# Attention and ternary FFN layer on one core: x's second part held behind wkv, wkv turned in two halves, six warming products

## The reference

```python
x = x + xattn(layernorm(x), ctx_512, Wq, Wkv_expand, Wout)   # 16 heads of 16, softmax, causal
x = x + ffn(layernorm(x), w_gate, w_up, w_down)
# xattn: qp = q @ Wq.T ; kv = ctx @ Wkv_expand.T ; k, v = split(kv) ; causal keeps the first 56 context rows
#        out = softmax(mask(qh @ kh.T / 4)) @ vh ; out @ Wout.T
# ffn:   w -> round(w / mean|w|) clipped to -1..1 ; activations -> round(x * 127 / max|x|) per token
#        down(silu(gate) * up), each product with ternary weights and integer activations
```

## Time and profile before

| | before |
|---|---|
| median of three runs | 96.84 us (96.61 to 97.01) |
| the profiled execution | 97.0 us, of which the span is 95.3 |
| PE / DVE / ACT / POOL busy in the span | 83% / 72% / 60% / 54% |
| first weight transpose of Wq on PE (wqT) starts | 8.03 us |
| scores of slot 0 start | 11.96 us |

### The profile page before, as it was taken

How to read it: one execution, slowest core, us unless ns; L and a number is a source line. 1 busy time by engine, 2 the same in 40 slices (tenths; PEclk the granted TensorE clock), 3 DMA queues, 4 the chain that set the end, 5 groups by cost and what they waited for, 6 DMA issues and landing times.

```text
span 95.3 us, 2459 instructions
## 1 busy us (share of the span) xinstructions
PE 79.4 (83%) x895; PEld 56.7 (60%) x895; DVE 68.4 (72%) x169; ACT 57.1 (60%) x103; POOL 51.4 (54%) x107
## 2 busy tenths in 40 slices
PE   4997796985999559999999997799945879998580
PEld 1365572855687548787977775766322547656370
DVE  4642847789592850798958999375999999999641
ACT  0622339493259973677587962586729387996610
POOL 5620271145945972397947962525186272587550
PEclk9999999999999999999999999999999999999999
DMA  1799999200000000000811826000000000011123
GB/s 18 195 327 363 349 353 393 86 0 0 0 0 7 3 0 7 0 7 7 187 33 30 197 68 152 0 7 0 0 0 0 0 0 0 9 57 55 55 98 122
DMA packets 11747, 7.59 MB, mean 80 GB/s; under 512 B 6552, under 2 KB 11480, under 8 KB 11736
## 3 DMA queue, kind: packets, MB, share of 16 engines
q1 hardware_dynamic: 11068, 6.93, 24.3%
q10 hardware_dynamic: 668, 0.51, 1.9%
HBM read 4.95 MB, written 0.92 MB: 62 GB/s over the span
## 4 chain that ended last, share of the span: by engine, by line
PE 45%; DVE 24%; ACT 12%; issue 8%; DMA 6%; ACTq 2%; POOL 1%; DVEq 0%
PE bank L889 26%; DVE amax L808 9%; PE sc L889 8%; DVE h_sb L801 7%; DMA wq_sb<-in_L_xattn_Wq_dram 6%; PE bank L1020 6%; ACT v_wide L560 4%; PE bank L1044 3%; ACT pT L375 2%; ACT k_wide L339 2%; ACT tern L587 2%; DVE s_tok L815 1%; ACT xnT L560 1%; DVE shifted L715 1%; ACTq L311 1%
## 5 line engine op out<-in xcount | busy, mean ns | idle before, releaser
L889 PE MATMUL sc<-wT,xqT 128*128 128x512 bf16 x56 | 13.9, 380 | 3.4 <-DVE h_sb L801 3.4
L300 POOL TENSOR_SCALAR wf_sb<-h_sb,r_tok 128x512 f32<-128x512 f32 x13 | 9.2, 718 | 10.4 <-DVE r_tok L822 10.4
L450 POOL TENSOR_SCALAR veps<-mv 128x1 f32<-128x1 f32 x13 | 2.5, 192 | 20.2 <-DVE mv L669 14.1
L607 ACT ACTIVATE wf_sb<-sc,s_out 128x512 f32<-128x512 f32 x14 | 9.6, 689 | 5.9 <-PE sc L889 3.6
L706 DVE TENSOR_REDUCE mx<-sc 128x16 f32<-128x896 f32 x8 | 8.7, 1090 | 3.8 <-PE sc L889 3.7
L801 DVE SCALAR_TENSOR_TENSOR h_sb<-sc,s_out,wf_sb 128x512 f32<-128x512 f32 x14 | 9.9, 740 | 1.1 <-ACT wf_sb L607 1.1
L889 PE MATMUL bank<-xnT,wqT 128*128 128x224 f32 (+1 forms) x40 | 7.4, 329 | 3.6 <-ACT xnT L560 2.2
L889 PEld LDWEIGHTS sc<-wT,xqT 128*128 128x128 bf16 x56 | 5.0, 98 | 9.2 <-DVE h_sb L801 5.1
L889 PEld LDWEIGHTS bank<-v_wide,pT 128*64 128x64 f32 x256 | 8.1, 138 | 2.3 <-issue 2.3
L889 PEld LDWEIGHTS bank<-xnT,wqT 128*128 128x128 f32 x40 | 6.2, 190 | 5.0 <-issue 3.4
L889 PE MATMUL bank<-v_wide,pT 128*64 128x34 f32 x256 | 9.0, 225 | 0.0
(11 more groups left out here) (107 smaller groups left out, 167.4 us busy)
## 6 DMA issues: line engine op xcount, KB each, us to landing
wf_sb<-in_L_ffn_w_gate_dram SPq DMA_DIRECT2D x1, 1024.0 KB, 9.2
wf_sb<-in_L_ffn_w_up_dram SPq DMA_DIRECT2D x1, 1024.0 KB, 11.5
wf_sb<-in_L_ffn_w_down_dram SPq DMA_DIRECT2D x1, 1024.0 KB, 11.9
out_dram<-k_wide SPq DMA_DIRECT2D x7, 128.0 KB, 1.7
x_sb<-in_x_dram SPq DMA_DIRECT2D x1, 512.0 KB, 6.7
x_sb<-in_x_dram SPq DMA_DIRECT2D x1, 256.0 KB, 5.6
wq_sb<-in_L_xattn_Wq_dram ACTq DMA_DIRECT2D x1, 256.0 KB, 5.7
wo_sb<-in_L_xattn_Wout_dram SPq DMA_DIRECT2D x1, 256.0 KB, 9.4
```

The source lines that it names most:

```text
L300: ops.tensor_scalar(h_int[:, t % 2, c, :], h_sb[:, t % 3, GC * c:GC * c + GC], r_tok[:, 1, t:t + 1], CODED, ALU.mult, ALU.add).then_inc(hi ...
L607: nc.scalar.activation(g_sb[:, t % 2, GC * c:GC * c + GC], SC[:, j % 4, :], ACT.Silu, scale=s_out[:, 0, t:t + 1]).then_inc(silu_ready, 1)
L889: return nc.tensor.matmul(*a, **k)
```

## The change

Four edits. SP waits until wkv has landed (`hold`) before it issues x1; everything behind x1 on SP's list waits with it. Job wkvT i turns columns 64i to 64i+63 of the identity's product with all four blocks, so that job 0 gives the K rows and job 1 the V rows; PE writes them into PSUM with a step of four elements, and the copy out is contiguous; the k jobs no longer wait for wkvT 1. PE starts with six warming products in place of nine. POOL builds the fp16 identity `ident_h` behind the first tile's power in place of ahead of it.

```diff
-WARM_PRODUCTS = 9
+WARM_PRODUCTS = 6
...
-SYNC_LOADS = ['x0', 'ctx0', 'ctx1', 'x1', 'x2', 'f0', 'wo0', 'f1', 'f2']
+SYNC_LOADS = ['x0', 'ctx0', 'ctx1', 'hold', 'x1', 'x2', 'f0', 'wo0', 'f1', 'f2']
...
+            if kind == "hold":
+                eng.wait_ge(wkv_in, 16)
+                return
...
             if kind == "wkvT":
-                last = copy(wkvT[:, :].rearrange("l (p o) -> l o p", o=4)[:, 2 * i:2 * i + 2, :],
-                            bank[:, 0:2 * P].rearrange("l (o p) -> l o p", o=2))
+                last = copy(wkvT[:, C * i:C * i + C], bank[:, 0:C])
...
-            link(nc.gpsimd.memset(ident_h[:, :], 0.0))
-            done(diagonal(ident_h[:, :], 0, P))
...
                 nc.gpsimd.tensor_tensor(rstd[:, t:t + 1], veps[:, t:t + 1], minus_half[:, 0:1],
                                         ALU.pow).then_inc(rstd_first, 1)
+            link(nc.gpsimd.memset(ident_h[:, :], 0.0))
+            done(diagonal(ident_h[:, :], 0, P))
...
-                    for o in range(2):
+                    for o in range(4):
                         for c in range(2):
-                            last = mm(bank[Q * c:Q * c + Q, P * o:P * o + P], wkv_sb[:, 2 * i + o, :], ident[:, :],
+                            last = mm(bank[Q * c:Q * c + Q, o:C:4], wkv_sb[:, o, :], ident[:, Q * i:Q * i + Q],
                                       start=True, stop=True)
...
-                    wait_read(pe, ("wkvT", 0), ("wkvT", 1), ("ctxT", 0), *[("ctxT", 1)] * (j1 > 2))
+                    wait_read(pe, ("wkvT", 0), ("ctxT", 0), *[("ctxT", 1)] * (j1 > 2))
```

## The result

The changed kernel takes 96.38 us in the median of 20 runs (95.55 to 96.91), the kernel before 96.88 in 20 runs beside it (96.51 to 97.52). The ratio, which is that of the means, is 0.9924, with a 95% interval of 0.9895 to 0.9952: 0.74 us faster, where 0.83 was forecast. The two medians are only 0.50 us apart, as the runs of both kernels spread over more than that. On the median of 96.84 that the forecast was made against, the ratio gives 96.1; forecast was 96.0.

The account below looks back on a forecast made before the run. Bound: wqT's start, where PE waited for Wq. wkvT to 5.4, products 0.80, ctxT 0.54, product 0.39, and Wq landing at 7.2, put wqT at 7.2 instead of 8.03; 96.84 - 0.83 = 96.0 us, range 95.4 to 96.9.

Parts of the forecast that it names:

- The 7.2 us for wqT: Start of wqT on PE: forecast at 7.2 us instead of 8.03, 0.83 us earlier.
- Wq lands at 7.2: Wq's load: without x1 sharing the transfer rate it saves 0.8 us and lands at 7.2 instead of 7.98.
- The clock rises at 4.6, as before: PE during wkvT: the clock reaches 2.4 GHz at 4.6 us, with 11 passes done by then.
- a clock that stays at 1.2 GHz behind the shorter row: PE after six warming products: ctxT at 7.25 instead of 6.62, so 97.5 us and more.
- wkvT's passes: wkvT on PE: 32 passes of 64 columns, 33 ns each at the fast clock and 66 at the slow one.
- the stepped rival: wkvT's PSUM write with a step of four bounds wkvT: wqT later than 8.03 above 65 ns a pass; chance within slower's 0.14.
- The last terms of the sum: PE between wkvT and wqT: three warming products 0.80 us, ctxT 0.54, one more product 0.39.
- The context at 6.2: Context load ahead of ctxT: lands at 6.2 us, taken between the 6.6 of before and 5.5.
- The costs of nothing: Contiguous copies (some 0.25 us on ACT and DVE each), k jobs' dropped wait and ident_h's later place: no effect on the time.
- nothing much moves: Ahead of wqT: context keeps its 6.6 us or x1 lands late; 0 to 0.48 us gained, 96.4 to 96.84; chance 0.21.
- slower: wkvT on PE: stepped write or slow clock delays wqT, 97.3 us at 80 ns a pass, 98.2 at 107; chance 0.14.
- more is saved: Context and Wq both land early, wkvT at 33 ns a pass: 1.0 to 1.25 us gained, 95.6 to 95.85; chance 0.15.

Follow-up runs that it names:

- e4: The kernel before with the hold alone added: 96.92 us, ratio 0.9986 to the kernel before.
- e5: The kernel before with six warming products in place of nine, nothing else: 97.02 us, ratio 1.0001 to the kernel before.
- e6: The kernel before with the hold and six warming products, wkvT as before: 95.98 us, ratio 0.9893 to the kernel before.
- e11: The changed kernel with wkvT 1 moved behind x's first tile and x1 issued ahead of the hold: 96.16 us, ratio 0.9921 to the kernel before.
- e8: The changed kernel without the four warming products between wkvT, ctxT and wqT: 95.01 us, ratio 0.9806 to the kernel before.
- e2: The changed kernel with nine warming products again: 96.70 us, ratio 0.9959 to the kernel before.
- e3: The changed kernel with wkvT written to PSUM without a step and the step put into the copies: 95.92 us, ratio 0.9908 to the kernel before.
- e9: The changed kernel with the hold waiting for Wq instead of wkv: 96.06 us, ratio 0.9891 to the kernel before.

## Why the prediction was right, and which terms were off

The result and the mechanism held: the wait for Wq is gone, x1's lateness is hidden, the gain of wqT reaches the end whole, and it takes both edits (e4, e5, e6). The 7.2 us for wqT, though, came out near the middle of what the runs show (6.65 to 8.0, read backwards) by errors that go against each other, so that the gain came so close to 0.83 is in part luck. The profiled execution even shows one of the prediction's own signs of being wrong: warming products 0.43 us apart behind wkvT; its wqT is at 8.00, hardly earlier than before.

*Wq lands at 7.2* was mis-sized: it is 5.9. The working took x1's 256 KB out of the way and left x2 and f0 where they were; the hold takes these away too (e11: x1 held or not is 1.1 of the 2.1 us). The even pair of legs that the sum showed was thus no such pair; the load was there 1.3 us before the 7.15 at which the sum has PE ready.

*The clock rises at 4.6, as before* was the wrong step on the other side. In the 14 profiles it was up as early as 4.0 (e8) and as late as 7 (both of the changed kernel), with nine products or six ahead. The late end gives wqT at 8.0; to the early one belongs the 6.65 of the fastest run, below the 7.15 of the sum. The case of "a clock that stays at 1.2 GHz behind the shorter row" did occur, but it isn't due to the shorter row, since e2 and e4 had it with nine. Its ctxT at 7.25 is what the profile shows (7.24), and yet the time is 96.88 and not 97.5: wqT follows 0.76 us behind ctxT, while the working had kept the 1.41 of before, in which the wait for Wq is contained. Whether the slowest runs of before (up to 97.5) come from a late clock too is not shown; its one profile has an early one.

*wkvT's passes* at 33 or 66 ns were too dear: 29 and 53. The prediction leaned a little (0.1 us) to the stepped rival and its rule; e3 and e8 show no cost of the step. The Trainium skill's sentence on non-contiguous patterns in "PSUM — Partial Sum Buffer", section Specifications, doesn't hold for this write: 53 ns a pass with a step of four elements and without.

*The last terms of the sum* were too long by 0.2 us: with the clock up and no load to wait for, three products take 0.75 and not 0.80 (5.90 to 6.65 in e9), and the one behind ctxT 0.22 and not 0.39, which has the modelled end in it.

*The context at 6.2* was cautious: in e8 PE was released by it at 5.2. *The costs of nothing* held: e6 without them has the gain. *x1* landed 2.7 us ahead of its reader in the changed kernel, instead of 0.4: it took 4.0 us from issue and not 5.6, and its reader came 0.75 us later than forecast. The two rivals "nothing much moves" and "slower" are out by their mechanisms; "more is saved" fits the times of the fastest runs (95.55 to 95.74) and the landings of Wq and the context, though not the median. That runs of this kernel lie within 0.4 us of each other was drawn from three of them: twenty of before spread over 1.0 us, twenty of the changed kernel over 1.4.

Why the clock doubles when it does stayed open: the profiles show only that it differs between executions, of kernels with the same products on PE up to then too (by 4.0 in e8, in the changed kernel about 7), and no run here controlled it.

## What to carry to other kernels

Two waits that end within half a microsecond of each other are one problem: neither the hold alone (0.9986) nor the earlier start alone (1.0001) moved the time by anything that can be told, the two together did (0.9893). Before a transfer is put off, look at what shares its rate; here loads with 2.8 us (x1) to 9.8 us (f0) to spare before their readers were taking a rate that the load PE waited for needed. And where runs of a kernel spread by more than the effect, find the point behind which the difference to the end is fixed (wqT here, 88.8 to 89.0 us): one profile then reads as one run, and what set the point's start in it says why.

## What the runs showed of the hardware

TensorE's clock went from 1.2 to 2.4 GHz anywhere between about 4.0 and 7 us from the start of the span, in programs that kept it busy from 1.27 on, while the granted clock in the rows of that stretch read 1.00 throughout. Four profiles with lists of one length up to wqT (the changed kernel twice, e3, e9) have wqT between 7.42 and 8.00 with no load waited for; that the 1.4 us between the runs of the changed kernel are the same thing is worked out from the sum of wqT and 88.9 and not seen. And a 256 KB load takes 2.7 us (x1 in e9, nothing ahead of it), 3.4 to 3.6 (Wq with the context ahead of it and x1 held), 4.7 (with x1 issued just before it) or 5.5 to 5.7 (with x1, x2 and f0 issued around it). A product of PE that writes every fourth float32 of its PSUM bank runs as fast as one that writes them side by side: 32 passes of 64 columns took 1.98 us either way at the lower clock.
